# A four-layer conditioned residual block on one core: the softmax shift per group of heads, with queries on partitions

## What is computed

```python
x = x + L0(x, f)   # 16 heads of 32: queries from f, keys and values from x,
                   # plus one "self" key and value per query, from f
x = x + L1(x, f)   # softmax(x' f^T) f
x = x + L2(x)      # adapter chosen per batch, then layernorm
x = x + L3(x)      # low-rank update chosen per batch
```

```python
q = (f + b_self) @ Wq + bq; k = cat([x + b_prev, f + b_self]) @ Wk + bk
score_prev = einsum('bhqd,bhkd->bhqk', q, k[:, :, :512]) * SCALE
score_self = (q * k[:, :, 512:]).sum(-1, keepdims=True) * SCALE
score_prev = where(mask, score_prev, -inf)
weights = softmax(cat([score_prev, score_self], -1))
attn = weights[..., :-1] @ v[:, :, :512] + weights[..., -1:] * v[:, :, 512:]
```

## Time and profile before

| | before |
|---|---|
| median of 3 runs | 1403.95 us (1402.32 to 1405.69) |
| the profiled execution | 1404.92 us |
| its span, first to last instruction | 1402.9 us |
| TensorE / VectorE / ScalarE / GpSimd busy | 1308.7 / 934.7 / 878.7 / 430.1 us |
| mean granted TensorE clock | 0.984 |

### The profile page before, as it was taken

One profiled execution on the slowest core, in us unless ns is written; L12 is line 12 of the kernel. 1 busy time (PEld: TensorE's weight loads), 2 busy tenths in 40 slices (PEclk: granted clock), 3 DMA queues, 4 the chain that ended last, 5 costly groups with the idle time before them and its releaser, 6 DMA issues.

```text
span 1402.9 us, 19927 instructions
## 1 busy us (share of the span) xinstructions
PE 1308.7 (93%) x7009; PEld 560.5 (40%) x7009; DVE 934.7 (67%) x1594; ACT 878.7 (63%) x1853; POOL 430.1 (31%) x372
## 2 busy tenths in 40 slices
PE   5798999899999999999998999999999999999995
PEld 1332364324543255332553335432454324533252
DVE  6286548874588646985569754896458864688544
ACT  2398545885468833887348864588536884388731
POOL 5341016510363105331064301651035310533114
PEclk8899999999999999999999999999999999999997
DMA  4222002130121302203012300313012130220200
GB/s 142 82 56 75 26 32 73 41 108 1 45 65 43 100 1 62 75 19 97 31 47 60 85 31 31 76 39 108 1 46 65 42 101 1 60 77 17 70 1 31
DMA packets 62161, 75.82 MB, mean 54 GB/s; under 512 B 14378, under 2 KB 35174, under 8 KB 62062
## 3 DMA queue, kind: packets, MB, share of 16 engines
q1 hardware_dynamic: 62062, 74.54, 18.7%
HBM read 40.81 MB, written 8.40 MB: 35 GB/s over the span
## 4 chain that ended last, share of the span: by engine, by line
PE 63%; ACT 19%; DVE 14%; issue 3%; DMA 1%; POOL 1%; SPq 0%; ACTq 0%; POOLq 0%
PE bank L441 23%; PE banks L441 12%; ACT banks L734 9%; DVE nmx L974 8%; ACT big L786 7%; PE bank L1319 6%; PE banks L1303 6%; PE bank L1164 6%; PE banks L1237 3%; PE bank L1266 2%; PE bank L1329 1%; PE bank L1271 1%; PE bank L1293 1%; DVE prod L964 1%; DVE y L1020 1%
## 5 line engine op out<-in xcount | busy, mean ns | idle before, releaser
L974 DVE TENSOR_REDUCE nmx<-banks 128x1 f32<-128x512 f32 x512 | 326.1, 684 | 71.8 <-PE banks L1237 70.7
L734 ACT ACTIVATE banks<-banks,nmx 128x512 f32<-128x512 f32 x512 | 340.1, 670 | 53.0 <-DVE nmx L974 50.4
L786 ACT ACTIVATE big<-banks 128x1024 f32<-128x1024 f32 x256 | 247.2, 1022 | 44.0 <-PE banks L1303 42.9
L441 PE MATMUL bank<-fT,w_hi 128*128 128x512 f16 x768 | 244.3, 379 | 1.1 <-issue 1.1
L1237 PE MATMUL banks<-KQ 97*128 97x512 f16 x512 | 154.3, 383 | 35.2 <-ACT banks L734 33.1
L516 POOL TENSOR_TENSOR big<-x,b2r 128x512 f32<-128x512 f32 x32 | 40.5, 1266 | 415.4 <-DVE x L909 375.3
L1303 PE MATMUL banks<-KQ 98*128 98x512 f16 x512 | 141.0, 382 | 13.7 <-ACT big L786 8.7
L441 PE MATMUL bank<-fT,w_lo 128*128 128x512 f16 x384 | 145.8, 380 | 0.0
L477 POOL TENSOR_TENSOR half<-qk,ones 128x512 f16<-128x512 f32 x64 | 66.5, 1039 | 238.6 <-ACT qk L716 238.6
L1319 PE MATMUL bank<-big,V 128*32 128x512 f32 x1024 | 136.4, 605 | 0.0
L441 PEld LDWEIGHTS bank<-fT,w_hi 128*128 128x128 f16 x768 | 74.8, 97 | 91.6 <-issue 15.3
(11 more groups left out here) (142 smaller groups left out, 1992.5 us busy)
## 6 DMA issues: line engine op xcount, KB each, us to landing
KQ<-half SPq DMA_DIRECT2D x384, 64.0 KB, 2.0
tiles_in<-in_x_dram SPq DMA_DIRECT2D x32, 256.0 KB, 7.3
tiles_in<-in_fside_BxSxS_dram SPq DMA_DIRECT2D x32, 256.0 KB, 2.7
x<-in_x_dram SPq DMA_DIRECT2D x8, 1024.0 KB, 5.7
out_dram<-x SPq DMA_DIRECT2D x32, 256.0 KB, 2.0
w<-in_L_cond_W_dram SPq DMA_DIRECT2D x16, 256.0 KB, 4.7
b2r<-in_L_cond_b_dram SPq DMA_DIRECT2D x8, 256.0 KB, 4.4
gr<-in_L_cond_gamma_dram SPq DMA_DIRECT2D x8, 256.0 KB, 5.6
```

The source lines that it names most:

```text
L441: mm = eng.matmul(out_ap, pairs[n][0], pairs[n][1], start=(first and n == 0), stop=(last and n == len(pairs) - 1))
L734: ins = eng.activation(bank(step, i)[:, j % 2, :], bank(step, i)[:, j % 2, :], ACT.Exp, bias=nmx[:, t, h:h + 1], accum_out=esum[:, t, h:h ...
L786: eng.activation(big[:, n % 2, 2 * u:2 * u + 2, :], bank(step)[:, :, :], ACT.Exp).then_inc(read(step), 1)
L974: eng.tensor_reduce(nmx[:, t, h:h + 1], bank(step, i)[:, j % 2, :], AX_X, ALU.max, negate=True).then_inc(max_done, 1)
```

## The change

- The shift is made per group, with queries on partitions. SELF is per group (bank 3, four times), ScalarE copies it negated (`self_rows`), TensorE transposes it (step SELFT), VectorE copies 16 columns per group into `nself`. NEG is gone.
- Step SHIFT follows each group's last SMAX: VectorE takes the minimum of `nmx` and `nself` (128x16, float16), transposes it in blocks of 32x32, and SP writes it into row 97 of `KQ` with four DMAs of 16 rows of 64 bytes. MROW is gone.
- Step DEN (where MROW stood): two differences of 128x64 on VectorE, one exponential of 128x128 on ScalarE.
- SROW: VectorE makes denominators, reciprocal and self weight on 128x64 tiles; then TensorE transposes the result (four transposes into bank 2, not 6), and VectorE splits it from PSUM into `norms16`, now one tile of 64 rows.
- `KQ` has group and side ahead of head, so the mask is written by four DMAs, not one. `head_rows` has twice the columns and 16 selects. SP waits for the split norms instead of `norms_done` before it loads x. Attention waits for each group's shift only.
- Maxima: still one reduction and one signal per 128x512 bank.

```diff
+DMAS_PER_SHIFT = (P // 32) * 16
+NR = 2 * H
+LOW_ROW = NR
+TJ = NT * NJ
...
             out.append(maxima.pop(0))
+            if not maxima or maxima[0][1] != out[-1][1]:
+                out.append(("SHIFT", out[-1][1]))
         elif not maxima and not rows:
-            out.append(("MROW",))
+            out.append(("DEN",))
...
-        if step == ("VS", 2):
-            later.setdefault(i + PARTS - 1, []).append(("NEG",))
+            later.setdefault(i + 2 * PARTS + 3, []).append(("SELFT", step[1]))
...
-        KQ = sb("KQ", [P, NJ, NG, 2, S], F16)
+        KQ = sb("KQ", [P, NG, 2, NJ, S], F16)
...
             for n, low in enumerate((0, LOW_ROW)):
-                for g in range(NG):
-                    v = head_rows32[:, g, :].rearrange("h (j d) -> h j d", j=NJ)
...
+                for r in range(2 * NG):
+                    v = head_rows32[:, r, :].rearrange("h (j d) -> h j d", j=NJ)
...
+                            for m in range(NG):
+                                eng.dma_start(KQ[MASK_ROW:MASK_ROW + 1, m, 0, :, :],
...
-                    elif step[0] == "MROW":
-
-                        wait_read(eng, step, b)
-                        eng.dma_start(KQ[SHIFT_ROW:SHIFT_ROW + 1, :, :, 1, :].rearrange("o j g n -> o (j g) n"),
-                                      shift[:, :]).then_inc(shift_in, 16)
+                    elif step[0] == "SHIFT":
+
+                        g = step[1]
+                        eng.wait_ge(shift_flip, b * NG + g + 1)
+                        rows = KQ[SHIFT_ROW:SHIFT_ROW + 1, g, 1, :, :].rearrange("o j (t m n) -> o (j t) m n", t=NT, n=32)
+                        for m in range(P // 32):
+                            eng.dma_start(rows[:, :, m, :], shiftT[32 * m:32 * m + TJ, g, :]).then_inc(shift_in[g], 16)
...
-                eng.wait_ge(norms_done, i + 1)
+                wait_read(eng, ("SROW",), i)
...
+                    elif kind == "DEN":
                         eng.wait_ge(self_diff, b * 2 + 2)
-                        eng.activation(self2[:, :, :], self2[:, :, :], ACT.Exp).then_inc(self_exp, 1)
+                        eng.activation(ediff[:, :, :, :], ediff[:, :, :, :], ACT.Exp).then_inc(self_exp, 1)
...
+                    elif kind == "SHIFT":
+                        g = step[1]
+                        eng.wait_ge(max_done, b * MAXIMA + (g + 1) * TJ)
+                        wait_read(eng, ("SELFT", g), b)
+                        eng.tensor_tensor(shift16[:, g, 0:TJ], nmx[:, g, :], nself[:, g, :], ALU.min
+                                          ).then_inc(shift_min, 1)
+                        eng.wait_ge(shift_min, b * NG + g + 1)
                         if tail:
...
+                            eng.wait_ge(shift_in[g], b * DMAS_PER_SHIFT)
+                        eng.transpose(shiftT[:, g, :], shift16[:, g, :]).then_inc(shift_flip, 1)
...
+                        eng.tensor_tensor(dens[:, :, :], esum[:, :, :], ediff[:, 0, :, :], ALU.mult).then_inc(den, 1)
+                        eng.wait_ge(den, b * 3 + 1)
+                        eng.tensor_tensor(dens[:, :, :], dens[:, :, :], ediff[:, 1, :, :], ALU.add).then_inc(den, 1)
+                        eng.wait_ge(den, b * 3 + 2)
+                        eng.reciprocal(nrm[:, :, :, 0, :], by_tile(dens[:, :, :])).then_inc(den, 1)
+                        eng.wait_ge(den, b * 3 + 3)
+                        eng.tensor_tensor(nrm[:, :, :, 1, :], nrm[:, :, :, 0, :], by_tile(ediff[:, 1, :, :]), ALU.mult
+                                          ).then_inc(norms_done, 1)
                         wait_full(eng, step, b)
...
+                        eng.tensor_scalar(norms16[0:NR, :], bank(step, i)[0:NR, :], RS, None, ALU.mult
+                                          ).then_inc(norms_hi, 1)
+                        eng.wait_ge(norms_hi, b + 1)
                         if tail:
 
                             eng.wait_ge(stored, b * NT * 16)
...
+                    elif kind == "SROW":
+
+                        eng.wait_ge(norms_done, b + 1)
                         wait_free(eng, step, b)
...
-                eng.wait_ge(shift_in, i * 16 + 16)
                 scores(0, i)
```

More of the change, by code:

```diff
@@ L165, in plan_banks @@
             m += 1
-        elif step[0] in ("MROW", "SROW"):
-            give({"MROW": 4, "SROW": 6}[step[0]], step)
-    for g in range(NG):
-        give(3, ("SELF", g))
+        elif step[0] in ("SELF", "SELFT"):
+            give(3, step)
+        elif step[0] == "SROW":
+            give(2, step)
     for g in range(NG):
@@ L386, in build_program @@
         mask_in = sem("mask_in")
-        shift_in = sem("shift_in")
+        shift_in = [sem(f"shift_in{g}") for g in range(NG)]
         max_done = sem("max_done")
-        MAXIMA = H * NT
-        self_neg = sem("self_neg")
+        MAXIMA = TJ * NG
+        shift_min = sem("shift_min")
+        shift_flip = sem("shift_flip")
         self_diff = sem("self_diff")
@@ L856, in _ @@
             for j in range(NJ):
[L857 to L859 removed]
+                eng.memset(head_cols[DH * j:DH * j + DH, j:j + 1], 1.0 / WS).then_inc(rows_ready, 1)
             eng.wait_ge(full[2], 1)
@@ L972, in mid @@
                         for j in (2 * q, 2 * q + 1):
-                            h = NG * j + g
-                            eng.tensor_reduce(nmx[:, t, h:h + 1], bank(step, i)[:, j % 2, :], AX_X, ALU.max,
+                            h = j * NT + t
+                            eng.tensor_reduce(nmx[:, g, h:h + 1], bank(step, i)[:, j % 2, :], AX_X, ALU.max,
                                               negate=True).then_inc(max_done, 1)
-                    elif kind == "MROW":
+                    elif kind == "SELFT":
+                        g = step[1]
@@ L979, in mid @@
                         wait_full(eng, step, b)
-                        wait_read(eng, ("SELF", NG - 1), b)
-                        if tail:
-                            eng.wait_ge(shift_in, b * 16)
-                        eng.tensor_tensor(shift[:, :], bank(step, i)[0:H, 0, :], self2[:, 0, :], ALU.min
-                                          ).then_inc(self_neg, 1)
-                        eng.wait_ge(self_neg, b + 1)
-                        eng.tensor_tensor(self2[:, 1, :], shift[:, :], bank(step, i)[0:H, 0, :], ALU.subtract
-                                          ).then_inc(read(step, i), 1)
@@ L1010, in mid @@
-                        eng.scalar_tensor_tensor(out=norms16[LOW_ROW:NROWS, :, :], in0=norms[:, :, :], scalar=RS,
-                                                 in1=norms16[0:H, :, :], op0=ALU.mult, op1=ALU.subtract
-                                                 ).then_inc(norms_lo, 1)
+                        eng.scalar_tensor_tensor(out=norms16[LOW_ROW:NROWS, :], in0=bank(step, i)[0:NR, :], scalar=RS,
+                                                 in1=norms16[0:NR, :], op0=ALU.mult, op1=ALU.subtract
+                                                 ).then_inc(read(step, i), 1)
@@ L1302, in scores @@
                     for j in (2 * u, 2 * u + 1):
-                        mm = eng.matmul(bank(step)[:, j % 2, :], KQ[0:SHIFT_ROW + 1, j, g, 0, k * P:(k + 1) * P],
-                                        KQ[0:SHIFT_ROW + 1, j, g, 1, :], start=True, stop=True)
+                        mm = eng.matmul(bank(step)[:, j % 2, :], KQ[0:SHIFT_ROW + 1, g, 0, j, k * P:(k + 1) * P],
+                                        KQ[0:SHIFT_ROW + 1, g, 1, j, :], start=True, stop=True)
                     mm.then_inc(done(step), 1)
```

147 lines of the change are left out of this document (70 added, 77 removed).

## The result

| | before | after |
|---|---|---|
| median of 4 runs each | 1404.52 us (1402.32 to 1405.69) | 1413.68 us (1412.71 to 1415.62) |
| ratio after to before, 95% interval | | 1.0069 (1.0051 to 1.0087) |
| the profiled execution, its span | 1404.92, 1402.9 us | 1412.71, 1410.9 us |
| TensorE / VectorE / ScalarE / GpSimd busy | 1308.7 / 934.7 / 878.7 / 430.1 us | 1309.2 / 899.8 / 872.9 / 433.2 us |
| granted TensorE clock | 0.984 | 0.985 |

A forecast was written before the change was run, and what follows sets the result against it. No engine bounds the whole; VectorE, then ScalarE, own the mixed stage's stretches. Seven stages at 0.7 us (+4.9) and the start (+3.8) give +8.7, 1413.6, less 1.0 for the median: 1412.6 us, range 1399 to 1420.

The forecast's parts named there:

- What is removed is free: Beside attention, nine VectorE instructions on 16 rows go, some 9 us per batch; their removal was costed at nothing.
- VectorE's stretch: Between the maxima where VectorE owns the chain: two copies and the shift of group 1 add 0.8 us per batch.
- ScalarE's stretch: Next part of the maxima: ScalarE gains 1.09 us, VectorE gets 1.1 more including 0.5 for port waits; set to zero.
- ScalarE's relief: Rival 1, mixed stages: dropping the negating copies saves 0.8 us a stage, total 1401.3, or 1395 with rival 2; chance 0.27.
- The end: Last maximum to attention: TensorE saves 0.6 us of transposes but waits 0.5 for the normalizers, net -0.1 us.
- Bank 2 and the late low halves: Attention's start: low halves wait for the last output store, done near 624.6, needed at 625.7; covered, nothing added.
- rival 3: Late norms: slow 64-byte shift DMAs, from 0.85 us each, delay bank 2 at attention's start; +22, 1435 us; chance 0.1.
- The self transposes: One more TensorE transpose per group, four of 0.11 us; three fall where TensorE waits anyway; counted zero.
- The start: Before the first batch: eight more GpSimd selects (3.4 us) and a larger zero fill (0.4) delay the fills, +3.8 us once.
- rival 2: At the start VectorE's cast gets in before GpSimd's first KQ fill: start -2.7 us, total 1406; chance 0.18.
- The sum: Whole kernel: 0.7 us per batch in seven stages (+4.9) and start +3.8, together +8.7; median 1412.6 us.

The follow-up runs named there:

- The kernel pair without blocks: Kernel before with fills behind the mask, norm piece and f splits later: 1380.52 us; changed kernel with these and normalizers one slot later: 1382.23 us.
- the extra minima: Changed kernel with six extra 128x16 minima on VectorE, behind the shift of group 1 in one kernel (1430.74 us), of group 0 in another (1411.10 us).
- the kernel with the later fills: Changed kernel with GpSimd's two fills of KQ rows 96 to 127 waiting until VectorE has made the mask: 1397.82 us, ratio 0.9957.
- six minima: Changed kernel with six extra 128x16 VectorE minima behind the shift of group 0: 1411.10 us, periods 166.90 us (-0.52).
- six minima behind group 1: Changed kernel with six extra 128x16 VectorE minima, each waiting for the one before, behind the shift of group 1: 1430.74 us, ratio 1.0192.

## Why the prediction was right, and where it was not

Forecast 1412.6 us, slower; measured 1413.68, within the range and slower. The mechanism held: what was taken from beside attention was worth nothing, and what was added between the maxima cost its length. By its steps:

- **What is removed is free**: right. The reciprocal shrank from 3.34 to 0.55 us and nobody noticed; VectorE's 35 us less are nowhere in the periods.
- **VectorE's stretch, +0.8**: right. Total +0.77 from the first maxima score to the end of that stretch; the instructions last 0.165 (copy, forecast 0.18), 0.17 (minimum, 0.33 once a stage) and 0.21 (transpose, forecast 0.2). The kernel pair without blocks gives 0.76, and the extra minima show that such instructions cost their length there. That the sum comes out so close is in part luck: the two copies count 0.09 each on the chain, and ScalarE's own copy of the self scores, about 0.16, is the rest. The forecast had counted that copy in the next stretch alone.
- **ScalarE's stretch, 0**: nearly. It was +0.17. The half microsecond that I added for port waits was not needed at the place I gave it: L995 at 611.24 took 0.33 and not 0.17 us, 0.16 of waiting. That ScalarE's relief is worth little is shown (0.15).
- **The end, -0.1**: right, -0.15. TensorE's wait was 0.28 and not 0.5.
- **Bank 2 and the late low halves, covered**: right in all seven full stages of the changed kernel's trace, with 0.9 us to spare in five and with 0.03 in the last. The shift DMAs took 0.60 us each (2.40 for four), under the 0.85 from which rival 3 decides. Their 64-byte rows cost nothing that shows: 1.7 us from issue to landing. But the cover is thin: when a store took 4.6 us to land, as in one stage of the kernel with the later fills, that stage became 3.1 us longer. The forecast took 2.0 us for the landing and left its spread out.
- **The self transposes, zero**: wrong by 0.12 a stage. I had said that three of the four fall where TensorE waits anyway, and did not charge the fourth. It falls at 562.28, ahead of the maxima, where TensorE has no gap, and pushes them back. Columns of the windows as above, changed kernel:

```profile
555.00:565.00 10.00, 10.00 (x60) 5.29 (x59) 7.74 (x14) 2.51 (x5) 8.58 (x8) 1.00 0.35 74
```

- **The start, +3.8**: 3.2, and shown by itself (3.13). Fill and selects did move what follows by 4.2, but a shorter load of Wo and shorter matmuls ahead of it gave back 0.5 each. That the cast might get in first (rival 2) did not happen: the fill started at 10.38 and the cast at 10.43, and it lasted 7.42 us.
- **The sum**: 0.92 a stage and not 0.7 (0.17 and 0.12 were left out), 3.2 and not 3.8 at the start. The two misses cancel in part (+1.5 and -0.6 us). The 9.6 that the marks give is 8.0 in the spans, since one stage of the profiled execution before was 1.3 us longer and the first 0.3.

What the prediction missed altogether is what its base had already lost to GpSimd: two blocked instructions in VectorE's stretch of each full stage and two at the start. Without them the kernel before takes 1380.52 us, 23 us less. The prediction named the mechanism twice (L932 and the cast) and used it for what the change adds, not for what was already lost.

## What to carry to other kernels

Moving a chain of instructions from 16 rows to 128 rows made it about three times shorter (9.3 to 3.1 us of VectorE's time), but ask first where each version of it lies: nine microseconds beside attention were worth nothing, and 0.8 us between the maxima cost 0.8. Look through the groups by line for a small instruction whose mean is far above its minimum, and see in the timeline what runs beside it: moving an instruction by one or two slots took it away. And compare a change in a repaired kernel too, for a cost that only a foreign block makes visible (3 us at the start here) is not the change's own. Last, when a change puts a buffer's release behind a DMA, look at the spread of its landings too, and not at the median alone.

## What the runs showed of the hardware

- A 48x512 or 64x1024 cast and an 8x512 tensor_scalar on VectorE took 6.27 to 7.42 us beside GpSimd's 32x8192 fill, and 0.42, 0.68 and 0.47 us without it: the fill writes only, so a writer alone blocks too.
- A 128x2 tensor_scalar took 1.00 to 1.06 us beside GpSimd's 128x512 splits and 0.16 to 0.17 without. Six 128x16 minima with two inputs in SBUF took 4.35 us beside such splits and 1.2 without.
- More work can make a stage shorter (six minima, -0.52 us) by missing a block.
- What TensorE's granted clock did after TensorE's longest wait between the maxima, in the seven full stages of a trace: it fell to half in three and in four of them after 1.84 us (two kernels), in three after 2.01 us (six minima behind group 1), in one after 1.65 us (the kernel before), in none after 1.37 us (the changed kernel) and in none after 1.00 us. A fall lasted 3.4 us (6.8 us after the wait of 4.41 us in the first batch). It cost 1.2 to 1.3 us in the first two kernels and the kernel before, and at most 0.15 us in the one with the minima, where VectorE is the limit.
- An output store of 256 KB landed 2.2 us after its issue in the median; the one that attention waits for took 4.6 and 4.3 us in one stage each of two traces.
- The block transpose of 128x32 in float16 takes 0.21 us. The reciprocal takes 3.34 us for 16x512 and 0.55 us for 128x64.
